# Layer-0 attention: PSUM banks shared two and two between scores and values, the turning of a group one slot later, the first half of the chain two slots later

## The chip, the cores and the metric

The kernel runs on one core of one Trainium2 chip. The metric is the device time of one launch in microseconds (us), the median over the runs shown. In the text PE is TensorE (matmuls), DVE is VectorE, ACT is ScalarE, POOL is GpSimd and SP is SyncE, which here only issues DMAs.

## The reference

A two-layer transformer over x of 4 batches by 512 tokens by 256 features, everything in float32. What bears on the change is layer 0:

```python
h = _layernorm(x, axis=-1) * (1 + ca) + sa
x = x + ga * _L0_attn_ref(h, Wq, Wkv, Wo)      # 16 heads of 16, one shared k and v, causal softmax
h = _layernorm(x, axis=-1) * (1 + cb) + sb
x = x + gb * _L0_ffn_ref(h, router_weight, router_bias, expert_bias)   # softmax over 64, top 8
```

Layer 1 follows (an attention with 16 heads of 128, and a gated feed-forward whose weights are gathered from a table of 16 values). The change does not touch it.

## The kernel before, in words

**Slots.** Layer 0's attention is one software pipeline, written out by hand. The work of a batch is cut into 44 units: four groups of four heads (`NG`, `HG`), and 11 units per group (`GU`), each a block of scores of up to 128x512 for one, two or four heads. All engines walk through the same loop `for s in range((NB - 1) * SLOTS0 + AFTER + CHAIN)`; each round is a slot, and `at(s, lag, length)` gives the unit that a step with this lag has in slot `s`. Each engine runs its own instructions strictly in this order and waits on semaphores.

For unit `i`, in the slots after its own: slot 0, PE computes scores into one of `S_BANKS` (lines 1257 and 1259) and DVE takes the row maxima (964). After a group's 11 units DVE turns the maxima (973 to 977), and SP's DMAs put them beside q, so that they take part in the next product. Slot 16 (`TURN`): PE computes the same scores turned (1239 and 1240) into bank 2 or 3, and ACT takes exp (727). Slot 18 (`VALUE`): behind the last unit of a key block, PE multiplies with the values (1270) into bank 5; four such steps fill the bank for a group. Slot 19: ACT copies the full bank to `oRaw` (735). Slot 20: PE turns `oRaw` back into bank 5 (1279), DVE divides by the row sums and writes `oTok` (983 and 987), and counts the semaphore `oev0`. The next group's first value product waits for `oev0`, since it writes bank 5.

**The chain.** When a batch's units are done, its rest runs in the slots of the next batch: `after0(n, b)`, n = 0 to 48, with n = 0 in slot `AFTER` = 63 of the batch. I call these chain slots. Chain slot 44 of one batch is chain slot 0 of the next, so chain slots 44 to 48 share slots with 0 to 4. The steps of before are: PE turns `oTok` (2, line 1185), ACT and DVE split it into a high and a low part (3 and 4, lines 668 and 887), PE multiplies with Wo (6 and 7), DVE applies the gate and adds to x (8 and 9, lines 892 and 894), the layer norm's statistics follow (10 to 13, lines 298 to 315), ACT normalises (14, line 326), PE turns (16, line 335), ACT scales and rounds (17 and 18), DVE makes the low part (19), PE computes the router (22 and 23), DVE adds the bias (24), ACT takes exp (25), DVE finds the top 8 (27 to 29, up to line 923), PE turns the weights (32, line 1211) and multiplies with the experts' biases (35, line 1219), DVE adds to x (36 and 37), and layer 1's norm follows: DVE 38 to 41, ACT 42, PE 44, ACT 45 and 46, DVE 47, and in 48 ACT issues two DMAs that store the result (705 and 706). The next batch's norm and q, k, v (`pre0`) run in other slots of the same loop.

**The banks.** Eight PSUM banks: scores 0, 1 and 4; turned scores 2 and 3; values 5; projections and the chain 6 and 7. A score matmul waits until the bank's last reader is done:

```python
S_BANKS = (0, 1, 4)
pe.wait_ge(max0, max(b * SLOTS0 + i - 2, 0))      # maxima of the unit three before
if k == 0:
    pe.wait_ge(oev0, b * NG + g)                  # the group before is in oTok
```

## Time and profile before

| what | value |
| --- | --- |
| median of 3 runs | 1391.39 us (1390.34 to 1394.19) |
| the profiled execution | 1389.02 us |
| its span, first to last instruction | 1387.2 us |
| PE busy | 1233.8 us, 89% |
| DVE busy | 961.9 us, 69% |
| ACT busy | 706.6 us, 51% |
| mean granted clock of PE | 0.937 |

The profile is of one execution of its own. Its time differs from the span by 1.82 us, which lies before the first and after the last instruction. Layer 0's attention with its chain takes the time from about 38 us to 395 us; layer 1 takes the rest.

### The profile page before, as it was taken

How to read it: one execution, taken by the hardware profiler on the slowest of the kernel's cores; microseconds unless marked ns; L12 is line 12 of the kernel's file. 1: busy time of each engine (PE TensorE's matmuls, PEld its weight loads, DVE VectorE, ACT ScalarE, POOL GpSimd, SP SyncE). 2: the span in 40 equal slices, each digit the busy share in tenths (PEclk: the TensorE clock that was granted, in tenths of full speed). 3: DMA queues.
4: the chain of work that ended last, by engine and by line, in shares of the span. 5: the costliest groups of instructions: out<-in, count | busy, mean ns of one | idle time of the engine just before them, and what ended most of it. 6: DMA issues, size and time to landing. Idle time of an engine off the chain costs nothing.

```text
span 1387.2 us, 24480 instructions
## 1 busy us (share of the span) xinstructions
PE 1233.8 (89%) x7708; PEld 949.9 (68%) x7708; DVE 961.9 (69%) x2821; ACT 706.6 (51%) x1639; POOL 551.8 (40%) x509
## 2 busy tenths in 40 slices
PE   6889888886479999999999999999998999996998
PEld 5535454443357787786777877878877788775887
DVE  5766777774576867878768778677668676674553
ACT  3354654555346546456455465465564564562442
POOL 0200000000048988898889888887603100000000
PEclk9799898888579999999999999999999999998999
DMA  6411011002010011101102101002002000000000
GB/s 216 122 36 46 25 35 55 24 32 92 30 66 12 31 39 72 40 1 41 41 10 94 36 8 39 31 15 96 15 19 79 16 30 30 0 0 1 16 16 31
DMA packets 31887, 56.76 MB, mean 41 GB/s; under 512 B 7096, under 2 KB 23328, under 8 KB 31312
## 3 DMA queue, kind: packets, MB, share of 16 engines
q1 hardware_dynamic: 27696, 42.93, 9.3%
q0 software_dynamic: 2976, 8.90, 2.2%
q10 hardware_dynamic: 1152, 4.19, 0.8%
q8 instruction: 26, 0.43, 0.1%
q14 instruction: 37, 0.30, 0.1%
HBM read 44.23 MB, written 11.66 MB: 40 GB/s over the span
## 4 chain that ended last, share of the span: by engine, by line
PE 56%; DVE 27%; issue 9%; ACT 5%; DMA 1%; SPq 1%; DVEq 0%; ACTq 0%
PE bank L1357 10%; PE bank L1335 8%; PE bank L278 7%; PE bank L280 6%; PE bank L279 6%; DVE qkst L1018 5%; PE bank L1346 4%; DVE qk L1037 4%; PE bank L1325 3%; PE bank L1270 2%; DVE negmax L964 2%; PE bank L1239 2%; ACT hN L326 2%; DVE negmax L1050 1%; PE bank L335 1%
## 5 line engine op out<-in xcount | busy, mean ns | idle before, releaser
L574 POOL TENSOR_SCALAR gtmp<-gidx,lut 128x344 f32<-128x344 int32 (+2 forms) x210 | 302.3, 1440 | 21.3
L577 POOL TENSOR_TENSOR gacc<-gacc,gtmp 128x344 f32<-128x344 f32 (+2 forms) x210 | 182.8, 870 | 17.5
L1335 PE MATMUL bank<-kT,qT 128*128 128x128 f32 (+3 forms) x512 | 179.5, 441 | 9.2 <-ACT probs L778 9.2
L1357 PE MATMUL bank<-pT,v 128*128 128x128 f32 x1280 | 155.4, 277 | 12.2 <-ACT pT L771 12.2
L778 ACT ACTIVATE probs<-bank,negmax 128x128 f32<-128x128 f32 (+3 forms) x256 | 135.7, 530 | 50.1 <-DVE negmax L1050 47.4
L1050 DVE TENSOR_REDUCE negmax<-bank 128x1 f32<-128x128 f32 (+3 forms) x256 | 123.4, 484 | 52.0 <-PE bank L1336 50.6
L1357 PEld LDWEIGHTS bank<-pT,v 128*128 128x128 f32 x1280 | 148.0, 192 | 15.9 <-DVE oL L1060 15.9
L964 DVE TENSOR_REDUCE negmax<-bank 128x1 f32<-128x512 f32 (+3 forms) x176 | 108.8, 635 | 68.2 <-PE bank L1259 67.3
L1018 DVE BATCH_NORM_STATS2 qkst<-qk 128x6 f32<-128x128 f32 x512 | 110.2, 281 | 64.0 <-issue 64.0
L278 PE MATMUL bank<-wgH,hL 128*128 128x512 f32 x384 | 152.9, 398 | 0.1
L280 PE MATMUL bank<-wgH,hH 128*128 128x512 f32 x384 | 152.9, 398 | 0.0
L279 PE MATMUL bank<-wgL,hH 128*128 128x512 f32 x384 | 152.4, 397 | 0.0
L771 ACT ACTIVATE pT<-bank 128x128 f32<-128x128 f32 (+3 forms) x256 | 111.1, 437 | 50.5 <-PE bank L1346 50.4
L567 POOL DMA_DIRECT2D gidx<-in_idx_gate x4 | 2.2, 540 | 335.1 <-DMA h_saved<-wft 335.1
L1045 DVE TENSOR_SCALAR probs<-probs,rsum 128x128 f32<-128x128 f32 (+3 forms) x256 | 124.1, 485 | 7.9
L757 ACT ACTIVATE qk<-bank 128x512 f32<-128x512 f32 x128 | 76.6, 599 | 98.9 <-PE bank L280 98.7
L1346 PE MATMUL bank<-identf,probs 128*128 128x128 f32 x640 | 112.7, 278 | 9.9 <-DVE probs L1045 6.7
L1346 PEld LDWEIGHTS bank<-identf,probs 128*128 128x128 f32 x640 | 69.9, 141 | 57.4 <-issue 28.0
L727 ACT ACTIVATE pT<-bank 128x384 f32<-128x384 f32 (+1 forms) x112 | 58.5, 535 | 84.1 <-PE bank L1240 78.9
L1037 DVE TENSOR_TENSOR qk<-qk,sm 128x512 f32<-128x512 f32 x128 | 98.2, 836 | 0.5
L1060 DVE TENSOR_TENSOR oL<-bank,oH 128x512 fp32r<-128x512 f32 x64 | 44.1, 689 | 74.5 <-ACT oH L785 74.3
L1335 PEld LDWEIGHTS bank<-kT,qT 128*128 128x128 f32 x512 | 77.3, 191 | 16.6 <-ACT probs L778 14.3
(215 smaller groups left out, 2713.6 us busy)
## 6 DMA issues: line engine op xcount, KB each, us to landing
hH<-h_saved SPq DMA_DIRECT2D x16, 512.0 KB, 3.9
hL<-h_saved SPq DMA_DIRECT2D x16, 512.0 KB, 4.6
qst<-q_parts SPq DMA_DIRECT2D x96, 64.0 KB, 2.3
wg<-in_wqkv SPq DMA_DIRECT2D x4, 1536.0 KB, 8.0
gate<-gates POOLq DMA_DIRECT2D x4, 512.0 KB, 7.4
wo<-in_wo SPq DMA_DIRECT2D x4, 512.0 KB, 8.9
out<-x SPq DMA_DIRECT2D x8, 256.0 KB, 2.1
wmod<-in_wmod SPq DMA_DIRECT2D x1, 1536.0 KB, 11.0
```

Of the source, the lines that this page charges most:

```text
L278: pe.matmul(o, wL, mH, start=start, stop=False)
L279: pe.matmul(o, wH, mL, start=False, stop=False)
L280: return pe.matmul(o, wH, mH, start=False, stop=stop)
L574: link(pool.tensor_scalar(tmp if j else acc, part, float(j), lut1[0:rows, j:j + 1], ALU.is_equal, ALU.mult))
L577: link(pool.tensor_tensor(acc, acc, tmp, ALU.add))
L964: dve.tensor_reduce(negmax[:, to:to + (heads - 1) * QT + 1:QT], bank[S_BANKS[(b * SLOTS0 + i) % 3]][:, 0:heads * w].rearrange("p (h k) -> ...
L1018: last = dve.bn_stats(qkst[:, u * HG + h, :], qk[:, u // 2, u % 2, h * HD1:(h + 1) * HD1])
L1037: dve.tensor_tensor(rows, rows, r.to_broadcast([P, HG, HD1]), ALU.mult).then_inc(qk_norm, 1)
L1050: dve.tensor_reduce(negmax[:, i:i + 1], bank[SCORE_BANKS[i % 3]][:, 0:n], AX.X, ALU.max, negate=True).then_inc(max1, 1)
L1335: pe.matmul(bank[SCORE_BANKS[i % 3]][:, 0:n], qT[:, h, t * P:n], kT[:, h, 0:n], start=True, stop=False)
L1346: last = pe.transpose(bank[5 + i % 2][:, k * P:(k + 1) * P], probs[:, i % 4, k * P:(k + 1) * P], identf[:, :])
L1357: last = pe.matmul(bank[7][:, t * P:(t + 1) * P], v1[:, k, h * HD1:(h + 1) * HD1], pT1[:, h % 2, at:at + P], start=(k == 0), stop=(k == t))
```

## The change

It does four things. (1) The third score bank, 4, becomes a second value bank: `S_BANKS = (0, 1)`, `V_BANKS = (5, 4)`, and groups alternate. A score matmul now waits for the maxima of the unit two before, and a group's first value product for the `oTok` of the group two before. (2) PE turns a group one slot later (`TAKEN` = 21, it was 20) and DVE writes `oTok` in slot 22; ACT's copy stays in slot 19. (3) The chain's first half comes two slots later, up to the router; the exp and norm of ACT are shifted by two or three, the top 8 by one. From chain slot 32 on nothing moves. (4) The wait for `cols_ready`, which guards bank 4's first use, goes from the third score to the second group's first value product.

```diff
-S_BANKS = (0, 1, 4)
+S_BANKS = (0, 1)
+V_BANKS = (5, 4)
 VALUE = TURN + 2
+TAKEN = VALUE + 3
...
-                if n == 3:
+                if n == 5:
                     act.wait_ge(y0_pe, b * 2)
...
-                        act.activation(oRaw[:, :], bank[5][:, :], ACT.Copy).then_inc(o_copied, 1)
+                        act.activation(oRaw[:, :], bank[V_BANKS[g % 2]][:, :], ACT.Copy).then_inc(o_copied, 1)
...
-                for i, b in at(s, VALUE + 2, SLOTS0):
+                for i, b in at(s, TAKEN + 1, SLOTS0):
                     if i % GU == GU - 1:
                         g = i // GU
                         dve.wait_ge(o_turned, b * NG + g + 1)
-                        pv = bank[5][:, :].rearrange("p (t h d) -> p t h d", t=QT, d=VW)
+                        pv = bank[V_BANKS[g % 2]][:, :].rearrange("p (t h d) -> p t h d", t=QT, d=VW)
...
-                    if b == 0 and i == 2:
-                        pe.wait_ge(cols_ready, 4)
-
-                    pe.wait_ge(max0, max(b * SLOTS0 + i - 2, 0))
-                    to = bank[S_BANKS[(b * SLOTS0 + i) % 3]][:, 0:heads * w].rearrange("p (h k) -> p h k", h=heads)
+                    pe.wait_ge(max0, max(b * SLOTS0 + i - 1, 0))
+                    to = bank[S_BANKS[(b * SLOTS0 + i) % 2]][:, 0:heads * w].rearrange("p (h k) -> p h k", h=heads)
...
                         g, k = i // GU, ENDS[i % GU]
+                        to = bank[V_BANKS[g % 2]]
                         if k == 0:
-                            pe.wait_ge(oev0, b * NG + g)
+                            pe.wait_ge(oev0, max(b * NG + g - 1, 0))
+                        if b == 0 and g == 1 and k == 0:
+                            pe.wait_ge(cols_ready, 4)
...
-                for i, b in at(s, VALUE + 2, SLOTS0):
+                for i, b in at(s, TAKEN, SLOTS0):
                     if i % GU == GU - 1:
...
-                            last = pe.transpose(bank[5][:, t * P:(t + 1) * P], oRaw[:, t * P:(t + 1) * P], identf[:, :])
+                            last = pe.transpose(bank[V_BANKS[i // GU % 2]][:, t * P:(t + 1) * P], oRaw[:, t * P:(t + 1) * P], identf[:, :])
```

The chain slots of `after0` move as the second hunk's does; in full:

| engine | step | before | change |
| --- | --- | --- | --- |
| PE | turn `oTok` | 2 | 4 |
| ACT, DVE | split it | 3, 4 | 5, 6 |
| PE, DVE | Wo; gate and add | 6, 7; 8, 9 | 8, 9; 10, 11 |
| DVE | norm | 10 to 13 | 12 to 15 |
| ACT | normalise | 14 | 17 |
| PE, ACT, DVE | turn; scale, round; low part | 16; 17, 18; 19 | 18; 19, 20; 21 |
| DVE | gate on `hN` | 20, 21 | 22, 23 |
| PE, DVE, ACT | router; bias; exp | 22, 23; 24; 25 | 24, 25; 26; 27 |
| DVE | top 8 | 27, 28, 29 | 28, 29, 30 |

No instruction is added or removed on any engine; only their order and the banks differ.

**PE, chain slot 44 of the first batch's chain.** L1279 (L1281 in the change) turns a batch's last group, L335 (L337) turns the rows of layer 1's norm, L1239 to L1259 (L1241 to L1258) are a slot's turned scores and scores. Before:

```order
L1257 MATMUL bank4<-kst,qst 128x256 x2
L1259 MATMUL bank4<-maskb,identb 128x2x128
L1279 MATMUL bank5<-identf,oRaw 128x128 x4
L335 MATMUL bank6<-identf,hN 128x128 x4
L335 MATMUL bank7<-identf,hN 128x128 x4
L1239 MATMUL bank2<-qst,kst 128x384
L1240 MATMUL bank2<-maskT,identb 128x128
```

In the change:

```order
L1256 MATMUL bank1<-kst,qst 128x256 x2
L1258 MATMUL bank1<-maskb,identb 128x2x128
L337 MATMUL bank6<-identf,hN 128x128 x4
L337 MATMUL bank7<-identf,hN 128x128 x4
L1241 MATMUL bank2<-qst,kst 128x384
L1242 MATMUL bank2<-maskT,identb 128x128
L1256 MATMUL bank0<-kst,qst 128x256 x2
L1258 MATMUL bank0<-maskb,identb 128x2x128
L1281 MATMUL bank4<-identf,oRaw 128x128 x4
```

The norm's eight matmuls now stand ahead of the group's turning, which comes a slot later and from another bank.

**ACT, at the second batch's chain.** L668 (L670) rounds the turned `oTok`, L705 and L706 (L707 and L708) issue the stores of the chain before, L727 (L729) is the exp of a slot. Before:

```order
L668 ACTIVATE oH0<-bank6 128x512
L668 ACTIVATE oH0<-bank7 128x512
L727 ACTIVATE pT0_1<-bank3 128x384
L705 DMA h1_saved<-hH 128x1024
L706 DMA h1_saved<-hL 128x1024
L727 ACTIVATE pT0_2<-bank2 128x512
```

In the change:

```order
L707 DMA h1_saved<-hH 128x1024
L708 DMA h1_saved<-hL 128x1024
L729 ACTIVATE pT0_2<-bank2 128x512
L670 ACTIVATE oH0<-bank6 128x512
L670 ACTIVATE oH0<-bank7 128x512
```

The two stores, with the wait for the low part ahead of them, now stand in front of the copies to `oH0`; before they stood behind.

**DVE, the first batch's layer norm.** L114 to L116 and L315 (L116 to L118 and L317) are the last steps of the norm, L973 to L977 (L975 to L979) the turning of a group's maxima, L964 (L966) the row maxima. Before, the end of the norm and what follows:

```order
L964 TENSOR_REDUCE negmax<-bank1 128x4
L114 TENSOR_TENSOR sm<-sm 128x4
L115 SCALAR_TENSOR_TENSOR sm<-sm 128x4
L116 SCALAR_TENSOR_TENSOR sm<-sm 128x4
L315 SCALAR_TENSOR_TENSOR sm<-mv,sm 128x4
L964 TENSOR_REDUCE negmax<-bank4 128x1
L973 CAST nmp<-negmax 128x16
L974 TENSOR_TENSOR nmp<-negmax,nmp 128x16
L977 STREAM_TRANSPOSE nmt<-nmp 128x32
```

In the change, a part in the middle of the norm:

```order
L966 TENSOR_REDUCE negmax<-bank1 128x1
L975 CAST nmp<-negmax 128x16
L976 TENSOR_TENSOR nmp<-negmax,nmp 128x16
L979 STREAM_TRANSPOSE nmt<-nmp 128x32
L116 TENSOR_TENSOR sm<-sm 128x4
L117 SCALAR_TENSOR_TENSOR sm<-sm 128x4
L118 SCALAR_TENSOR_TENSOR sm<-sm 128x4
L116 TENSOR_TENSOR sm<-sm 128x4
L117 SCALAR_TENSOR_TENSOR sm<-sm 128x4
L118 SCALAR_TENSOR_TENSOR sm<-sm 128x4
L966 TENSOR_REDUCE negmax<-bank0 128x1
```

The turning of the maxima was behind the norm's last instruction and now lies inside the norm.

## Rows read from the trace of the kernel before

**Rows 1.** Page of before: the span, TensorE's busy share, TensorE's granted clock in 40 slices.

```profile
span 1387.2 us, 24480 instructions
...
PE 1233.8 (89%) x7708; PEld 949.9 (68%) x7708; DVE 961.9 (69%) x2821; ACT 706.6 (51%) x1639; POOL 551.8 (40%) x509
...
PEclk9799898888579999999999999999999999998999
```

**Rows 2.** Busy time by stretch: us from:to, length, engines' busy us, PEclk, DMA share, GB/s.

```profile
80.00:117.50 37.50, 34.18 (x270) 19.06 (x268) 25.86 (x53) 22.72 (x43) 0.00 (x0) 1.00 0.13 36
...
199.50:271.30 71.80, 59.06 (x424) 32.30 (x424) 52.35 (x145) 36.66 (x77) 0.00 (x0) 0.86 0.12 38
...
215.60:228.10 12.50, 8.42 (x61) 4.01 (x57) 11.88 (x39) 5.77 (x12) 0.00 (x0) 0.81 0.05 15
```

**Rows 3.** Who waited for whom, 38 to 345 us: total us, times, longest us.

```profile
PE bank L1279 <- ACT oRaw L735: 14.8, 12, 6.0
...
PE bank L1270 <- DVE oTok L987: 6.9, 5, 1.9
...
PE bank L335 <- ACT hN L326: 5.3, 3, 1.8
...
PE bank L1257 <- DVE negmax L964: 4.1, 6, 1.5
```

**Rows 4.** TensorE in time order, 199 to 231 us: start, us, engine, line; idle before, releaser.

```profile
199.66 1.12 PE L1279 MATMUL bank<-identf,oRaw 128*128 128x128 f32 x4 [2.72 <-ACT oRaw L735]
...
210.78 0.39 PE L278 MATMUL bank<-w0H,oL 128*128 128x256 f32 x1 [1.06 <-DVE oL L887]
...
218.22 0.66 PE L1279 MATMUL bank<-identf,oRaw 128*128 128x128 f32 x4 [0.34 <-ACT oRaw L735]
...
222.14 1.06 PE L1270 MATMUL bank<-probs,vS 128*32 128x512 f32 x8 [1.91 <-DVE oTok L987]
...
228.10 1.97 PE L335 MATMUL bank<-identf,hN 128*128 128x128 f32 x8 [1.84 <-ACT hN L326]
```

**Rows 5.** TensorE in time order, 86 to 107 us, a turning.

```profile
91.80 0.66 PE L1279 MATMUL bank<-identf,oRaw 128*128 128x128 f32 x4 [0.34 <-ACT oRaw L735]
```

**Rows 6.** ScalarE in time order, 264 to 272 us: normalised rows, then the group's copy.

```profile
268.35 2.07 ACT L326 ACTIVATE hN<-x,sm 128x256 f32<-128x256 f32 x4 [3.44 <-DVE sm L315]
...
270.81 0.58 ACT L735 ACTIVATE oRaw<-bank 128x512 f32<-128x512 f32 x1
```

**Rows 7.** TensorE in time order, 210 to 218.5 us: first matmul of slots 8 and 10.

```profile
214.46 0.39 PE L1239 MATMUL bank<-qst,kst 98*128 98x512 bf16 x1
...
216.59 0.39 PE L1239 MATMUL bank<-qst,kst 98*128 98x512 bf16 x1
```

**Rows 8.** ScalarE in time order, 205 to 229 us: issues of the two stores.

```profile
208.96 0.39 ACTq L705 DMA_DIRECT2D h_saved<-hH  x1
209.38 0.49 ACTq L706 DMA_DIRECT2D h_saved<-hL  x1
```

**Rows 9.** VectorE in time order, 215 to 227 us: start and end of its long run.

```profile
215.64 0.68 DVE L892 TENSOR_TENSOR ytmp<-bank,gate 128x512 f32<-128x512 f32 x1
...
220.79 0.67 DVE L964 TENSOR_REDUCE negmax<-bank 128x2 f32<-128x512 f32 x1
...
225.72 0.16 DVE L315 SCALAR_TENSOR_TENSOR sm<-mv,sm 128x4 f32<-128x4 f32 x1
...
226.40 0.16 DVE L973 CAST nmp<-negmax 128x16 bf16<-128x16 f32 x1
...
226.81 0.21 DVE L977 STREAM_TRANSPOSE nmt<-nmp 128x32 bf16<-128x32 bf16 x1
```

**Rows 10.** TensorE in time order, 218 to 224 us: a score matmul with its mask.

```profile
219.62 0.40 PE L1257 MATMUL bank<-kst,qst 96*128 96x128 bf16 x4
```

**Rows 11.** VectorE in time order, 240 to 259 us: end of the top-8 work.

```profile
249.46 0.43 DVE L923 TENSOR_TENSOR ex<-ex,rsm 128x260 f32<-128x260 f32 x1
```

**Rows 12.** TensorE in time order, 240 to 275 us: turning of the routing weights.

```profile
251.14 0.60 PE L1211 MATMUL bank<-identf,ex 128*65 128x128 f32 x4
```

More of the change, by code:

```diff
@@ L676, in after0 @@
                     norm_f0.act_mod(act, b)
-                elif n == 18:
+                elif n == 20:
                     act.wait_ge(h1_stored, b * 32)
                     norm_f0.act_high(act, b, hH)
-                elif n == 19 and last:
+                elif n == 21 and last:
                     split_w1(0, 0, 3 * KT)
-                elif n == 25:
+                elif n == 27:
                     act.wait_ge(r_nmax, b + 1)
@@ L883, in after0 @@
                 last = b == NB - 1
-                if n == 4:
+                if n == 6:
                     for k in range(KT):
@@ L894, in after0 @@
                     ch.step(dve.tensor_tensor(xb(b, 2 * t2, 2), xb(b, 2 * t2, 2), ytmp[:, :, :], ALU.add))
-                elif n in (10, 11, 12, 13):
-                    for part in (2 * (n - 10), 2 * (n - 10) + 1):
+                elif n in (12, 13, 14, 15):
+                    for part in (2 * (n - 12), 2 * (n - 12) + 1):
                         norm_f0.dve_part(part, dve, ch, b)
-                elif n == 19:
+                elif n == 21:
                     norm_f0.dve_low(dve, b, hH, hL)
-                elif n in (20, 21):
-                    rows = hN[:, 2 * (n - 20):2 * (n - 20) + 2, :]
+                elif n in (22, 23):
+                    rows = hN[:, 2 * (n - 22):2 * (n - 22) + 2, :]
                     ch.mark(dve.tensor_tensor(rows, rows, gate(gate0, 1, b).to_broadcast([P, 2, D]), ALU.mult))
-                elif n == 24:
+                elif n == 26:
                     dve.wait_ge(r_pe, b + 1)
@@ L924, in after0 @@
                                       ALU.mult).then_inc(r_w, 1)
-                elif n == 30 and last:
+                elif n == 31 and last:
                     split_w1(0, slice(0, 3 * KT))
@@ L1269, in _ @@
                         for h in range(HG):
-                            last = pe.matmul(bank[5][h * VW:(h + 1) * VW, k * P:], vS[:, b * QT + k, :], pT0[k][:, h, :],
+                            last = pe.matmul(to[h * VW:(h + 1) * VW, k * P:], vS[:, b * QT + k, :], pT0[k][:, h, :],
                                              start=(k == 0), stop=(k == QT - 1))
                         last.then_inc(pv0, 1)
-                for i, b in at(s, VALUE + 2, SLOTS0):
+                for i, b in at(s, TAKEN, SLOTS0):
                     if i % GU == GU - 1:
```

30 lines of the change are left out of this document (15 added, 15 removed).

## The prediction

> **What bounds the kernel now.** The page comes first [rows 1]. PE is busy for 89% of 1387.2 us, but its granted clock reads 9 in nearly all slices from the thirteenth on and 5 to 8 in eight of the first twelve. The change lies wholly in the first 395 us, so I read that part by stretches [rows 2]. From 80 to 117.5 us, where no chain runs yet, PE is busy for 34.18 of 37.50 us at clock 1.00: there PE bounds. From 199.5 to 271.3 us, one batch of slots with a chain beside it, PE is busy for 59.06 of 71.80 us at clock 0.86, DVE for 52.35, ACT for 36.66. No engine is full. Something in turn bounds, so the waits are next.
>
> The list of waits [rows 3] shows what the change aims at: PE waited 14.8 us for ACT's copy `oRaw` ahead of the turning, 6.9 us for `oTok` ahead of a value product, and 5.3 us for normalised rows. For the third score bank's reader, `negmax`, it waited only 4.1 us. Of the 14.8 us one wait is 6.0 long and lies in the tail, where the last batch has nothing to run beside it.
>
> Where each wait sits decides what it is worth. In time order [rows 4] I see three sorts. (a) A turning waits 0.34 us because the copy was issued only one slot before. (b) At 199.66 us the turning waits 2.72 us: it is chain slot 44, ACT was held by the norm and the copy stands behind it. (c) At 222.14 a value product waits 1.91 us for `oTok`, and at 228.10 PE waits 1.84 us for normalised rows. Sort (c) lies in a stretch in which DVE is busy for 11.88 of 12.50 us [rows 2]: from the gate at 215.64 to the end of the norm at 225.88 (225.72 + 0.16) DVE runs without a gap [rows 9], and PE is busy for 8.42 us only. There DVE bounds, and a shorter wait at one place comes back at the next.
>
> **The change part by part.**
>
> (1) *Turning one slot later, early groups.* Two groups are turned between 80 and 117.5 us, with 0.34 us of wait each, of which one is shown [rows 5]. PE bounds there, so 2 x 0.34 = 0.7 us go. Of the other seven short waits three lie in DVE's long run and are worth nothing; the rest are inside the balance of the chain below.
>
> (2) *Chain slot 44.* The norm's turning now precedes the group's. ACT ends the normalising at 270.42 (268.35 + 2.07) and the copy at 271.39 (270.81 + 0.58) [rows 6]. PE may go on 1.0 us sooner; what is left of the wait is for the normalised rows. This place occurs twice (199.7 and 271.4 us) outside the tail. In the tail the same 1.0 us is gained before `oH0`, but there the stores now precede `oH0` on ACT (below, 0.9 us), so I count the tail at zero.
>
> (3) *The first half of the chain, two slots later.* For one period I add up how much later the first Wo product and the gate behind it come. Two more slots precede them: from the start of chain slot 8 to that of 10 PE took 216.59 - 214.46 = +2.1 us [rows 7]. The wait for `oL0`, -1.06 [rows 4], goes, since DVE's low part of the other chain no longer stands right ahead of it. On ACT the two stores, 0.39 + 0.49 = +0.9 [rows 8], now stand ahead of the copies to `oH0`, and the slot's exp behind these. That makes 2.1 - 1.06 + 0.9 = +1.9. What queues behind the stores is one exp and the copies; PE's turned scores wait for that exp.
>
> (4) *The turning of the maxima inside the norm.* It took DVE from 226.40 to 227.02 (226.81 + 0.21), 0.6 us [rows 9], behind the norm; now it lies inside, so the norm ends +0.6 later. SP's DMAs of the maxima are no later by slots.
>
> (5) *What is given back.* From slot 32 on nothing moved, so two slots less lie between the norm's turning and the weights' turning (L1211). If only PE counted, -2.1 would come back, and with them a part of ACT's wait on its exps. A limit is the router's chain. The top 8 ended at 249.89 (249.46 + 0.43) [rows 11], L1211 began at 251.14 [rows 12]: slack 1.25 us. The bounds are thus -1.25 (slack alone) and -3.0 (both slots, the 0.34 at the turning and some 0.5 of better packing on ACT). I take -2.6, nearer the full return, because the router's scores leave the slots in which DVE also had the second group's `oTok`.
>
> (6) *Two score banks.* Unit s now waits for the maxima of s - 2. In DVE's long run this binds: the score matmul at 219.62 [rows 10] was issued while the maxima two units before ended at 221.46 (220.79 + 0.67) [rows 9], so it will start 1.8 us later. But PE then waited until 222.14 for `oTok`, a wait that is gone. The one takes the place of the other, value 0. Outside DVE's run I allow +0.2 per period; bounds 0 and the 1.84 us of this one instance. `cols_ready` costs nothing, since the columns are copied long before the second group's values. The first twelve units, which start behind DVE's opening work, are bound by DVE at either depth: 0, at most +0.4.
>
> *The sum.* Full period: -1.0 + 1.9 + 0.6 - 2.6 + 0.2 = -0.9, twice: -1.8. The first period (117.5 to 199.5 us) has neither the wait at 44 nor the stores nor the wait for `oL0`: +2.1 + 0.6 - 2.6 + 0.2 = +0.3. With (1): -1.8 + 0.3 - 0.7 = **-2.2 us**. The profiled execution took 1389.02 us, so it would be 1386.8; the median of the runs shown is 2.37 higher, so for the median 1391.39 - 2.2 = **1389.2 us**. A measurement of this kernel tells about 0.3%, 4.2 us, from no change. So I forecast no difference that can be told.
>
> *A rule against the trace.* The trace says that most of the wait for `oTok` sits where DVE bounds [rows 2, 4] and is worth nothing. The Trainium skill (Perfetto Trace Analysis, Matmuls) says that independent matmul groups should rotate through different PSUM banks, so that the reading of one overlaps the next group. By that rule the values gain a rotation and the scores keep a shorter one. By the trace the sum has 0 for this, by that rule -6.9. The trace agrees that the values stood still behind one bank; it cannot show the scores with two.
>
> **The rivals.**
>
> *PE was the bound after all, faster.* If the waits that bank 5 causes are worth their face, this happens: 6.9 us for `oTok`, the waits before the turnings outside the tail, 14.8 - 6.0 = 8.8, together 15.7 us [rows 3]; PE would further hold its full clock longer. Half of it, as DVE covers half, gives 1391.4 - 7.9 = 1383.5 us. For it: PE is the busiest engine in the period (59.06 against 52.35) and at the lower of its two levels (1.2 GHz) for part of the time, which a steadier feed would change; 0.81 in the long run is where it waits. Against it: DVE's run without a gap, which the change lengthens. The rule named above would bring the time out this way. Chance 0.30.
>
> *The two slots aren't given back, slower.* The mechanism: the chain to the top 8 is a serial one, router, bias, exp, top 8. If it takes all the slots that it has, PE stands before L1211 for what the first half lost. The price per period: (3) + (4) = +2.5, less the slack of 1.25, = +1.3, plus the score banks' full +1.84, less 1.0 at slot 44 in two of three: 3 x 3.1 - 2.0 - 0.7 = +6.7, 1398.1 us. It decides when less than about 2 us return, and more so if score waits leave DVE without work after its run. For it: fourteen slots now lie between the norm's turning and L1211 where sixteen were, and each holds maxima of 0.6 us beside the chain's DVE work. Against it: DVE was busy only 52.35 of 71.80. Chance 0.22.
>
> **How the numbers follow.** The forecast, no difference that can be told, has 0.48 around 1389.2, its own range 1386 to 1394. The rival on the fast side has 0.30, the one on the slow side 0.22. Each spreads a little over the bound at 1387.2 or 1395.6: faster by over 0.3% 0.33, within 0.3% 0.45, slower 0.22. The range for 8 in 10 reaches from 1382.5 (the fast rival and 1 us) to 1397.5 (nearly the slow one).
>
> **What would show it.** In the changed profile the turnings' waits for `oRaw` should be near nothing outside the tail, and those for `oTok` gone. In their place PE's waits for `negmax` grow from 4.1 to some 10 us, most of them in DVE's long run, which stays about 11 us long with the turning of the maxima inside. At chain slot 44 PE waits for normalised rows 1.0 us less than it did for the copy. The wait of PE before L1211 (none now) becomes 0 to 1.5 us. The period from one chain slot 44 to the next stays within 1 us of 71.8. I would be wrong if DVE's run shows gaps, if the wait before L1211 is over 2 us, or if the clock of the period leaves 0.84 to 0.88.

## Result and the profile after

| what | before | change |
| --- | --- | --- |
| median | 1391.09 us (6 runs, 1390.25 to 1394.19) | 1398.87 us (6 runs, 1397.28 to 1399.76) |
| ratio, 95% interval | | 1.0051 [1.0038, 1.0063] |
| the profiled execution, its span | 1389.02, 1387.2 us | 1397.76, 1396.0 us |
| layer 0's last store issued, from the span's start | 393.7 us | 398.9 us |

The change makes the kernel slower, by 7.8 us or 0.51%. That is more than the 4.2 us that can be told from nothing, and it lies outside the range of the prediction (1382.5 to 1397.5).

The page of the change, against [rows 1] (TensorE's clock in the last row):

```profile
span 1396.0 us, 24479 instructions
...
PE 1230.8 (88%) x7708; PEld 941.1 (67%) x7708; DVE 965.9 (69%) x2821; ACT 705.7 (51%) x1639; POOL 552.3 (40%) x509
...
PEclk8799988998579999999999999999999999998999
```

The span is 8.8 us longer, PE is busy for 3.0 us less and DVE for 4.0 more. Neither engine's work has grown by what the span has, so most of the loss is waiting. The stretches that answer to [rows 2] (length, then PE, PEld, DVE, ACT and POOL busy, then PEclk, DMA share and GB/s):

```profile
80.00:117.50 37.50, 35.17 (x286) 18.47 (x278) 26.78 (x55) 24.67 (x48) 0.00 (x0) 1.00 0.13 35
204.50:276.30 71.80, 59.25 (x431) 31.43 (x428) 53.17 (x145) 36.37 (x75) 0.00 (x0) 0.90 0.11 37
```

From 80 to 117.5 us, where no chain runs, PE is busy for 35.17 us where it was for 34.18, with 286 matmul records for 270: it gets through more work in the same time. In a period (204.5 us is 5 us behind 199.5, as the change is at that place) PE is busy for 59.25 us as before (59.06), but at clock 0.90, where it was 0.86. The list of waits from 38 to 345 us, against [rows 3]:

```profile
PE bank L1256 <- DVE negmax L966: 28.1, 32, 1.9
...
PE bank L1241 <- DMA qst<-nmt: 7.3, 6, 1.7
...
PE bank L337 <- ACT hN L328: 7.0, 3, 5.5
...
PE bank L337 <- DVE rsm L910: 1.8, 1, 1.8
```

The 14.8 us for `oRaw` and the 6.9 for `oTok` are gone from the list, as intended. The waits for `negmax` rose from 4.1 to 28.1, far more than the 10 forecast. The 7.3 us for the DMA of the maxima (`nmt`) are no larger than before, where that row, which did not stand among those shown, reads 7.5. The sum alone doesn't tell where these waits lie, and one has moved to a costly place. The list therefore doesn't explain the loss. What does is to follow the ends of the same steps through both traces. Read from TensorE's rows, in us, as the end of the step's last matmul, the change less before (before's own time in the second column):

| end of the step | before | change | late chain, old banks | Wo in slot 7 | hFA later | both repairs | norm turned first |
| --- | --- | --- | --- | --- | --- | --- | --- |
| chain 1: Wo | 136.2 | +3.5 | +4.3 | +0.6 | +3.6 | +0.8 | +0.6 |
| chain 1: router | 162.7 | +4.3 | +5.7 | +3.5 | +4.4 | +3.0 | -1.1 |
| chain 1: weights turned | 173.6 | +6.3 | +8.8 | +6.9 | +1.8 | +0.5 | -1.0 |
| chain 1: norm turned (slot 44) | 202.5 | +5.0 | +8.8 | +6.3 | +0.5 | -2.5 | -3.6 |
| chain 2: Wo | 214.6 | +10.2 | +13.3 | +7.5 | +6.5 | -1.1 | -0.3 |
| chain 2: router | 241.2 | +11.0 | +14.1 | +10.4 | +6.2 | +1.8 | -3.1 |
| chain 2: weights turned | 251.7 | +8.6 | +11.8 | +8.9 | +3.8 | -0.6 | -3.1 |
| chain 2: norm turned (slot 44) | 274.3 | +5.8 | +11.6 | +6.9 | +1.9 | -3.4 | -4.9 |
| chain 3: Wo | 286.4 | +9.0 | +16.4 | +7.9 | +7.2 | -3.2 | -4.1 |
| chain 3: router | 313.0 | +8.7 | +16.8 | +10.4 | +7.7 | -1.0 | -4.6 |
| chain 3: weights turned | 322.0 | +5.9 | +14.0 | +7.9 | +5.3 | -3.8 | -4.6 |
| layer 0: last norm turned | 390.7 | +5.2 | +14.9 | +7.2 | +3.7 | -4.5 | -6.6 |

(The last five columns are the experiments `c_late_chain`, `h_wo7`, `j_pre3`, `k_pre3_wo7` and `m_turn_after`, below. Each column is one execution, and executions of one kernel differ: those of the controls q_before_wo7 and r_before_pre3, whose medians can't be told from before's, end layer 0 4.0 and 4.3 us ahead of before's. So a sum down a column says little to within some 4 us; a step that recurs in many executions says more.)

Two places stand out. **Up to Wo** the change loses 5.2 us in chain 2 (from +5.0 to +10.2) and 3.2 in chain 3; some 2.1 of that are the two slots that now precede Wo, and are due back later. **From the router to the turning of the weights** it gives back 2.4 and 2.7 us in chains 2 and 3, as forecast, but loses 2.0 in chain 1.

A second table leaves the moved steps out. The mask's matmul of a slot's turned scores (L1240, L1242 in the change) is in the same slot in every version. How much longer than in before it took from one such matmul to another, in us, in one execution of each:

| chain, slots | change | a | c | f | h | j | k | m | q | r |
| --- | --- | --- | --- | --- | --- | --- | --- | --- | --- | --- |
| chain 2, 5 to 11 | +2.5 | 0.0 | +2.5 | +2.5 | 0.0 | +2.5 | +0.1 | +1.6 | -0.2 | 0.0 |
| chain 3, 5 to 11 | +1.0 | +1.5 | +2.5 | +2.5 | +0.1 | +1.0 | +0.1 | 0.0 | -0.3 | 0.0 |
| chain 1, 11 to 25 | -0.6 | -1.6 | -0.1 | +3.8 | -0.7 | -0.6 | -1.4 | -1.6 | -1.1 | -1.1 |
| chain 2, 11 to 25 | -0.7 | -2.8 | -0.7 | +3.4 | -0.7 | -1.7 | -0.7 | -2.8 | +0.2 | -2.3 |
| chain 1, 25 to 35 | +5.6 | +1.2 | +6.7 | +1.0 | +8.5 | +1.9 | +1.9 | 0.0 | 0.0 | +1.1 |

(The letters are the experiments below.) The first row of the change, from before's slots 5 and 11, then its own: 10.28 us became 12.77.

```profile
207.04 0.27 PE L1240 MATMUL bank<-maskT,identb 128*128 128x256 bf16 x1
...
217.32 0.22 PE L1240 MATMUL bank<-maskT,identb 128*128 128x128 bf16 x1
```

```profile
212.60 0.27 PE L1242 MATMUL bank<-maskT,identb 128*128 128x256 bf16 x1
...
225.37 0.22 PE L1242 MATMUL bank<-maskT,identb 128*128 128x128 bf16 x1
```

*The first place.* TensorE of the change in time order, around chain slot 8 of the second chain (start, us; in brackets the idle time before and its releaser):

```profile
206.40 1.06 PE L337 MATMUL bank<-identf,hN 128*128 128x128 f32 x8 [0.41 <-ACT hN L328]
...
216.04 0.22 PE L1258 MATMUL bank<-maskb,identb 128*128 128x128 bf16 x1
217.92 0.39 PE L1241 MATMUL bank<-qst,kst 98*128 98x512 bf16 x1 [1.66 <-DMA qst<-nmt]
...
219.51 0.58 PE L280 MATMUL bank<-w0H,oL 128*128 128x256 f32 x1
...
222.03 0.28 PE L282 MATMUL bank<-w0H,oH 128*128 128x256 f32 x1
222.15 0.39 PE L1241 MATMUL bank<-qst,kst 98*128 98x512 bf16 x1
```

PE has finished the slot's last score matmul at 216.26 us and waits until 217.92, because the turned scores of chain slot 8 are the first of a group (unit 11 plus the turn's 16 slots) and need the maxima that SP's DMAs bring. Behind them stands Wo. In before, Wo stood ahead of this wait, in slots 6 and 7. VectorE's turning of the maxima, of before and of the change:

```profile
207.54 0.21 DVE L977 STREAM_TRANSPOSE nmt<-nmp 128x32 bf16<-128x32 bf16 x1
```

```profile
212.22 0.21 DVE L979 STREAM_TRANSPOSE nmt<-nmp 128x32 bf16<-128x32 bf16 x1
```

In the change they are turned at 212.43 (212.22 + 0.21) and usable at 217.92, 5.5 us later. In before they were turned at 207.75; 5.5 us on would be 213.2, when PE was at Wo (210.78 to 214.6), and the turned scores at 214.46 [rows 7] waited for nothing. Wo covered this wait, and the change has pulled the cover away. After the wait the clock is low as well. The granted clock is the third number from the end; first the change, then before at Wo:

```profile
216.20:219.50 3.30, 1.64 (x14) 0.45 (x12) 1.87 (x4) 1.60 (x4) 0.00 (x0) 0.86 0.65 211
219.50:222.10 2.60, 2.60 (x16) 2.59 (x12) 0.00 (x0) 0.00 (x0) 0.00 (x0) 0.52 0.07 24
222.20:224.60 2.40, 2.40 (x25) 1.86 (x24) 0.56 (x1) 0.60 (x1) 0.00 (x0) 1.00 0.00 0
```

```profile
210.80:214.40 3.60, 3.60 (x28) 3.25 (x28) 1.67 (x3) 0.86 (x2) 0.00 (x0) 1.00 0.52 203
```

PE was busy for 1.64 of 3.30 us, the clock was granted at 0.86, and then Wo's first half ran at 0.52, nearly all at the lower level of 1.2 GHz. Its twelve products took 2.64 us (219.51 to 222.15), where in before they took 1.53 (210.78 to 212.31) at 1.00: +1.1. The Trainium skill (TensorE: Matmul & The Clock Gate, A second HAM failure mode) reports such falls for a kernel that cycled through PSUM banks with small idles between groups; here the trace agrees that an idle stood ahead of the fall, but the idle is for a DMA and not for a bank.

The fall is not a fixed companion of the wait. In all profiles, chains 2 and 3, Wo's first half ran at a clock of 0.50 to 0.67 in eight of ten places where Wo stood in slots 8 and 9, at 0.51 to 0.68 in four of sixteen where it stood in 6 and 7, and at 1.00 in all ten where it stood in 7 alone. In chain 3 of the change it ran at 1.00, and there slots 5 to 11 cost 1.0 us in place of 2.5. So the lost cover costs 1.0 us by itself, and 1.5 more where the clock falls.

*The second place.* Chain 1 meets the q, k, v norm of batch 3 (its steps are `pre0`; `hA` and `hFA` are its tiles; L345 scales it, L687 is the router's exp). First ScalarE, then VectorE, then TensorE of the change:

```profile
170.78 0.60 ACT L729 ACTIVATE pT<-bank 128x512 f32<-128x512 f32 x1 [2.95 <-PE bank L1242]
171.27 1.44 ACT L345 ACTIVATE hFA<-bank,modc 128x512 f32<-128x512 f32 x2
172.60 0.35 ACT L687 ACTIVATE ex<-lg,rsm 128x64 f32<-128x64 f32 x1
```

```profile
168.67 0.42 DVE L910 TENSOR_REDUCE rsm<-lg 128x4 f32<-128x256 f32 x1
...
174.06 0.61 DVE L914 MAX8 top<-ex 128x8 f32<-128x64 f32 x4 [1.70 <-ACT ex L687]
```

```profile
169.35 1.07 PE L337 MATMUL bank<-identf,hA 128*128 128x128 f32 x8 [1.77 <-DVE rsm L910]
...
179.22 0.65 PE L1213 MATMUL bank<-identf,ex 128*65 128x128 f32 x4 [0.61 <-DVE ex L925]
```

In before, ScalarE at the same place:

```profile
165.13 0.34 ACT L685 ACTIVATE ex<-lg,rsm 128x64 f32<-128x64 f32 x1
...
167.31 1.44 ACT L343 ACTIVATE hFA<-bank,modc 128x512 f32<-128x512 f32 x2
```

In before the exp (165.13) stood ahead of `hFA` (167.31). In the change the router's maximum, DVE's L910, is two slots later. PE's turning of `hA`, which uses the chain's banks and so waits for it, loses 1.77 us; the units behind it come late; ACT scales `hFA` first and takes the exp at 172.60, 3.5 us after the maximum was there (168.67 + 0.42); and DVE waits 1.70 us for it. On unmoved work the change loses 5.6 us there, from slot 25 to 35, and 1.1 and 0.1 us in the same slots of chains 2 and 3. No other chain meets these steps: only chain 1, the first batch's, has a batch's `pre0` begin in its slots 26 to 29, and that is batch 3's.

### The profile page after: what moved, and what is told of

Same layout as the page of the kernel before. It is cut to its first block, busy times and chain, and to the rows that moved or that the text cites. A ratio compares the mean times of both kernels' runs of the same rounds, so it can differ in the third digit from the quotient of the medians.

```text
span 1396.0 us, 24479 instructions
## 1 busy us (share of the span) xinstructions
PE 1230.8 (88%) x7708; PEld 941.1 (67%) x7708; DVE 965.9 (69%) x2821; ACT 705.7 (51%) x1639; POOL 552.3 (40%) x509
## 4 chain that ended last, share of the span: by engine, by line
PE 53%; DVE 29%; issue 10%; ACT 5%; DMA 1%; SPq 1%; DVEq 0%; ACTq 0%
PE bank L1359 10%; PE bank L1337 7%; PE bank L280 7%; PE bank L281 6%; PE bank L282 6%; DVE qkst L1020 4%; DVE qk L1039 4%; PE bank L1348 4%; PE bank L1327 2%; DVE negmax L966 2%; PE bank L1272 2%; DVE negmax L1052 1%; PE bank L1256 1%; PE bank L1241 1%; PE bank L337 1%
## 5 line engine op out<-in xcount | busy, mean ns | idle before, releaser
L966 DVE TENSOR_REDUCE negmax<-bank 128x1 f32<-128x512 f32 (+3 forms) x176 | 109.7, 638 | 69.8 <-PE bank L1258 68.6
L729 ACT ACTIVATE pT<-bank 128x384 f32<-128x384 f32 (+1 forms) x112 | 59.2, 538 | 79.3 <-PE bank L1242 72.1
L1256 PE MATMUL bank<-kst,qst 96*128 96x512 bf16 (+3 forms) x256 | 69.1, 323 | 28.6 <-DVE negmax L966 28.1
```

The lines of the kernel that those rows point to most:

```text
L966: dve.tensor_reduce(negmax[:, to:to + (heads - 1) * QT + 1:QT], bank[S_BANKS[(b * SLOTS0 + i) % 2]][:, 0:heads * w].rearrange("p (h k) -> ...
```

## The experiments

All times are medians; the ratio is to runs of before that were measured beside it, with its 95% interval. In the expectations, LATE CHAIN holds the chain's slots to blame, TWO SCORE BANKS the waits for `negmax`, PHASE the clock; COVER is the first place above, ROUTER and COLLISION are theories of the second.

**a_old_chain.** The change's banks and later turning, the chain in its old slots. The diff, against the change, shows two of the steps; all go back.

```diff
-                if n == 5:
+                if n == 3:
...
-                elif n in (8, 9):
+                elif n in (6, 7):
```

> The change with its banks and its later turning, but the chain in the slots of before. Theory LATE CHAIN (the two slots and what they collide with cost the time): the cost is gone and the gain at chain slot 44 stays, 1386 to 1390 us, at or under before (1391.1). Theory TWO SCORE BANKS (the scores' shorter rotation costs it): 1396 to 1399 us, as the change. Theory PHASE (layer 1 took 3.6 us more in the profile, by when TensorE's clock fell): 3 us or more of any difference lies behind 400 us of the profile.

Measured: 1391.93 us (12 runs), 0.9994 [0.9981, 1.0008]. The loss is gone; the gain expected on top of that, 1386 to 1390, can't be seen in the time. Banks and turning alone do nothing that can be told, in spite of this row of its waits:

```profile
PE bank L1256 <- DVE negmax L966: 27.6, 34, 1.9
```

**b_two_score.** Only the third score bank taken away; of the diff the banks are shown, and the score's wait goes with them, from i - 2 to i - 1.

```diff
-S_BANKS = (0, 1, 4)
+S_BANKS = (0, 1)
```

> Before with two score banks and nothing else; bank 4 stands idle. TWO SCORE BANKS: slower by 4 to 7 us, 1395 to 1398. LATE CHAIN: within 1.5 us of before, with at most 2 us lost in the first 60 us of slots, where the profile of the change shows the scores waiting for maxima.

Measured: 1393.39 us (12 runs), 1.0011 [0.9995, 1.0027]. At most some 3.8 us, and the best value is 1.4.

```profile
PE bank L1257 <- DVE negmax L964: 24.0, 36, 1.9
```

PE waits 24.0 us for `negmax`, 20 more than before, and the time moves by 1.4: the waits stand where DVE or something behind it bounds anyway. TWO SCORE BANKS falls.

**c_late_chain.** Before with the change's chain slots, banks and turning as they were; of the diff against before one step is shown.

```diff
-                if n == 3:
+                if n == 5:
```

> Before with the chain's first half in the slots of the change, banks and turning as before. LATE CHAIN: slower by 4 to 7 us, 1395 to 1398, and in the profile the router's exp of the first chain stands 3 us behind the maxima it needs, since ACT has the next batch's scaling ahead of it. TWO SCORE BANKS: 1390 to 1392.

Measured: 1404.37 us (6 runs), 1.0083 [1.0065, 1.0101]. The later chain alone costs 12.3 us, more than the whole change and twice what was expected. With it, banks and turning give some 4.5 us (by the ratios) to 5.5 us (by the medians) back, which without it are worth nothing.

**d_ex26.** The change, with ACT's router exp one slot earlier (27 to 26), ahead of `hFA`.

```diff
-                elif n == 27:
+                elif n == 26:
                     act.wait_ge(r_nmax, b + 1)
```

> The change with ACT's router exp at chain slot 26, where it stands ahead of the scaling for batch 3. LATE CHAIN: 3 us less than the change, 1395.5 to 1396.5, all of it between 168 and 180 us of the profile. TWO SCORE BANKS: within 1 us of the change (1398.9).

Measured: 1400.35 us (6 runs), 1.0055 [1.0037, 1.0073]. A miss: no gain at all. The exp of chain 1 came 4 us sooner than in the change (168.54 for 172.60), but the top 8 began only 1.1 sooner and the weights were turned 0.4 sooner. I take it that this puts right only what follows PE's wait for the maximum, not that wait.

**e_wo_old** and **h_wo7.** The change with Wo ahead of the DMA's wait again: in e with all its steps from the turning of `oTok` to Wo in their old slots, in h with only the two halves of Wo in slot 7.

```diff
-                elif n in (8, 9):
+                elif n == 7:
                     pe.wait_ge(ot_lo, (b + 1) * KT)
-                    for t in (2 * (n - 8), 2 * (n - 8) + 1):
+                    for t in range(QT):
```

> The change with the turning and splitting of oTok and the Wo products back in chain slots 2, 3, 4, 6 and 7; gate, norm and router stay late. Theory COVER (Wo in slots 6 and 7 filled the wait for the DMAs of the maxima, which gate slot 8's turned scores; in 8 and 9 it stands behind that wait): most of the 7.8 us comes back, 1391 to 1394 us. Theory ROUTER (the loss is made where the late router meets the norm of batch 3 and the top 8): 1397 to 1399 us. Theory PLAIN (each of the two slots costs its own work before Wo, and only that): 1394 to 1396 us.

> The change with both halves of Wo in chain slot 7, ahead of the turned scores that wait for the DMAs; nothing else moves, oTok is still turned in slot 4. COVER: 4 us or more less than the change, at or under 1395 us, and the wait for the DMAs at slot 8 is gone from the second and third chain. PLAIN and ROUTER: within 1.5 us of the change, 1397.5 to 1400.

Measured: e 1396.59 us, 1.0038 [1.0022, 1.0053]; h 1396.77 us, 1.0038 [1.0022, 1.0054] (12 runs each). Both lie some 2 us under the change, which their intervals alone don't separate from it, and in no range that a theory had named: less than COVER's, more than the others'. The traces show the mechanism. TensorE of h, where Wo begins, and its waits for that DMA:

```profile
219.05 0.38 PE L280 MATMUL bank<-w0H,oL 128*128 128x256 f32 x1 [0.85 <-DVE oL L889]
```

```profile
PE bank L1242 <- DMA qst<-nmt: 3.1, 3, 1.1
```

The wait for the DMA (L1242 in h is the change's L1241) falls from 7.3 to 3.1 us, and from slot 44's norm to Wo the second chain loses 1.3 us instead of 5.2. On unmoved work slots 5 to 11 cost 0.0 and 0.1 us in chains 2 and 3, in place of 2.5 and 1.0. Most of it was lost again elsewhere: chain 1's slots 25 to 35 cost 8.5 us in h for 5.6 in the change, and the gate, which reads Wo's product, still had its slots behind 9. Why the collision was dearer here is open.

**f_router_old** and **i_wo7_router.** The change (f) and h (i) with router, bias, exp and top 8 in their old slots.

```diff
-                elif n in (24, 25):
+                elif n in (22, 23):
                     norm_f0.wait_ready(pe, b)
```

> The change with router, bias, exp and top 8 back in slots 22 to 29; everything up to the low part stays late. ROUTER: 1391 to 1395 us, and in the profile the first chain's exp no longer falls behind. COVER: at most 3 us less than the change, 1396 to 1399 us.

> Both: Wo in slot 7 and the router in its old slots, banks and later turning as in the change. If COVER and ROUTER both hold, they add up: 1388 to 1392 us, at or under before. If only one holds, as the better of the two runs alone.

Measured: f 1405.32 us, 1.0104 [1.0079, 1.013] (6 runs); i 1399.38 us, 1.0054 [1.0028, 1.008] (7 runs). ROUTER's price falls, and i's forecast with it: f is slower than the change. From Wo to the turning of the weights the change gives 1.6 us back in chain 2; f loses 1.7 there and i 4.1, and chain 1 is no better than in the change (+2.7 in f for +2.8). The second table shows why. The collision itself is gone in f: slots 25 to 35 of chain 1 cost 1.0 us where they cost 5.6. But from slot 11 to 25 f loses 3.4 to 3.8 us in each chain, where the change loses none: the router now stands right behind the low part that it reads, and PE waits for it, a wait that the change doesn't have:

```profile
PE bank L280 <- DVE hL L357: 3.2, 3, 1.1
```

That wait is 1.1 us a chain; where the rest of the 3.4 to 3.8 goes is not followed. An early router thus cures the second place at a higher price. The difference of f and i, 5.9 us, is a second measure of COVER, in medians.

**j_pre3** and **k_pre3_wo7.** The change with batch 3's steps on `hFA` two slots later; k has Wo in slot 7 besides.

```diff
-                if n == 2:
+                if n == (4 if b == NB - 1 else 2):
...
-                elif n == 3:
+                elif n == (5 if b == NB - 1 else 3):
...
-                if n == 4:
+                if n == (6 if b == NB - 1 else 4):
...
-                if n == 1:
+                if n == (3 if b == NB - 1 else 1):
```

> The changed kernel; only the last batch's q, k, v norm, which runs beside the first chain, has its steps on hFA moved two slots later (PE's turning of norm_a0 1 to 3, ACT's scaling and rounding 2, 3 to 4, 5, DVE's low part 4 to 6). COLLISION theory (in the change these steps meet the router's maximum and exp, which moved two slots, and cost the first chain its give-back of about 4.4 us): some 3 to 4.5 us less than the change, about 1394.5 to 1396, and the distance from the first chain's router to its turning of the weights falls from 2.0 us more than before to about 2 us less. If the give-back is missing for another reason (the slots there are not filled by TensorE): no change from 1398.9.

> The same as j_pre3, and both halves of the Wo product in chain slot 7 instead of 8 and 9. If COVER (Wo stands ahead of the wait for the DMA of the maxima, as before, worth about 2 us by the earlier run) and COLLISION are two separate costs, they add: 1392 to 1394. If they are the same time seen twice: about the better of the two alone, 1394.5 to 1396.5.

Measured: j 1393.01 us, 1.0008 [0.9993, 1.0022]; k 1389.01 us, 0.9990 [0.9977, 1.0004] (12 runs each). Against 1398.87 these are -5.9 and -9.9 us (by the ratios -6.0 and -8.5), more than expected of either, and j's and k's intervals lie wholly under the change's. From j to k, measured side by side, Wo's place is worth 4.0 us by the medians and 2.5 by the ratios. In j, ScalarE and TensorE at the second place:

```profile
169.15 0.35 ACT L687 ACTIVATE ex<-lg,rsm 128x64 f32<-128x64 f32 x1 [0.58 <-DVE rsm L910]
...
171.61 1.44 ACT L345 ACTIVATE hFA<-bank,modc 128x512 f32<-128x512 f32 x2
```

```profile
174.73 0.65 PE L1213 MATMUL bank<-identf,ex 128*65 128x128 f32 x4 [0.46 <-DVE ex L925]
```

The exp is back ahead of `hFA`; ScalarE waits 0.58 us for the maximum and starts as soon as it is there, and the weights are turned 4.5 us sooner than in the change (174.73 for 179.22). From router to weights chain 1 now gives 2.6 us back (+4.4 to +1.8 in the table), as the others did in the change. COLLISION holds. In k chain 2's Wo stands at -1.1 where it stood at +10.2.

**m_turn_after** and **n_last_late.** Two ways to have the norm turned ahead of the last group at chain slot 44 in the kernel before. In m PE does a slot's chain step before its group turning; in n only the last group is turned, and written to `oTok`, a slot later. The expectation of m says that it differs only at chain slot 44. That is not so: a group is turned in chain slot 22 as well, and there m puts the first half of the router ahead of it.

```diff
+                for n, b in at(s, AFTER, CHAIN):
+                    after0(n, b)
                 for i, b in at(s, VALUE + 2, SLOTS0):
...
-                for n, b in at(s, AFTER, CHAIN):
-                    after0(n, b)
```

> The kernel before; on TensorE the turning of a group stands behind the chain's step of the same slot instead of ahead of it. This differs only at chain slot 44, where layer 1's norm is then turned ahead of the batch's last group. It takes this one part out of the change. By the prediction's step (2): 1.0 us less at each of two places, and the same once in the tail, so 1388.5 to 1390.5 against 1392. By the change's profile, in which this segment came out 2.6 us shorter: up to 5 us less, 1387. If the gain at slot 44 needs the later slot as well: no difference.

> The kernel before; only a batch's last group is turned, and written to oTok, one slot later (three banks for scores, one for values, chain in its old slots). The 2.7 us wait for the copy at chain slot 44 goes, and what is left is the wait for the normalised rows. By what the change gained at this place (2.6 us, twice outside the tail): 1387 to 1389 against 1392. By step (2) of the prediction (1.0 us, twice): about 1390. If the next group's first value product, which then waits for oTok one slot longer, takes the gain back: 1391 to 1393.

Measured: m 1386.89 us, 0.9964 [0.9951, 0.9978] (13 runs); n 1390.64 us, 0.9993 [0.9979, 1.0008] (12 runs). m is faster than both kernels, by 4.9 us than before. TensorE at chain slot 44, of m, then of before; and the stretches' granted clock, of m (the last at its second chain's Wo), then of before, then of the change:

```profile
197.76 1.06 PE L335 MATMUL bank<-identf,hN 128*128 128x128 f32 x8 [1.85 <-ACT hN L326]
198.66 1.06 PE L1284 MATMUL bank<-identf,oRaw 128*128 128x128 f32 x4
```

```profile
200.57 1.91 PE L335 MATMUL bank<-identf,hN 128*128 128x128 f32 x8
```

```profile
197.70:199.30 1.60, 1.54 (x11) 1.51 (x12) 1.53 (x3) 1.37 (x3) 0.00 (x0) 0.82 0.04 10
199.30:202.00 2.70, 2.70 (x15) 1.59 (x14) 2.19 (x5) 1.81 (x4) 0.00 (x0) 0.50 0.00 0
...
208.90:211.60 2.70, 2.69 (x12) 2.62 (x12) 1.16 (x2) 0.30 (x1) 0.00 (x0) 0.51 0.63 250
```

```profile
199.60:202.30 2.70, 2.64 (x13) 2.58 (x14) 2.24 (x5) 0.49 (x2) 0.00 (x0) 0.50 0.02 6
```

```profile
206.40:208.30 1.90, 1.90 (x18) 1.78 (x19) 1.83 (x4) 1.87 (x5) 0.00 (x0) 1.00 0.04 9
```

The wait is 0.87 us shorter (1.85 for 2.72 [rows 4]), near the 1.0 forecast. The clock adds nothing here. In before the eight matmuls of the norm took 1.91 us, at 0.50, in m 1.06, at 0.82; but in m the full fall to 0.50 comes right behind them, on the work that before did at 0.90. On unmoved work, from chain slot 39 to slot 5 of the next chain, m gains 0.8 us and n, whose wait is the same 1.85, 0.9: the wait and no more. By slot 11 both have lost 1.6 us again, because the clock is low at Wo's first half too (0.51 in m), behind the same wait of 1.06 us for `oL0` after which before's stood at 1.00.

What m has and n has not is the turning in slot 22. From slot 21 to 23 m gains 0.52 us in each of the three chains, 1.6 in all, and so does s, which has the same edit; n gains nothing there. By these parts, two places of 0.85 us and three of 0.52, m's edit is worth some 3.3 us and what the tail adds, and n's 1.7; at the second slot 44, though, the traces with this order spread from -2.7 to +0.4 us with the clock. m's profile is of its fastest run, 1378.43 us, 8.5 under its median, so its column overstates.

**o_late_fixed, q_before_wo7, r_before_pre3, s_best.** Do the two repairs undo what the later chain did, or help any kernel? o has both on c_late_chain, q and r one each on before. s is m with r's edit.

> The kernel before (three banks for scores, one for values, turning in its old slot) with the change's chain slots, and both repairs: Wo's two halves in chain slot 7, the last batch's steps on hFA two slots later. Without repairs this kernel took 1404.4. If COVER and COLLISION are what a later chain costs with any banks: it loses about what the change lost by the two repairs, 9.9, so 1394 to 1396, with the rest above before from the copy at chain slot 44 that is still waited for. If the repairs need the second value bank or the later turning: 1398 or more.

> A control: the kernel before with both halves of Wo in chain slot 7 (they stood in 6 and 7, both ahead of the wait for the maxima's DMA already). If the gain of this repair in the change comes from the order against that wait: no gain here, 1391 to 1394. If two halves in one slot are better by themselves: 1388 to 1390.

> A control: the kernel before with only the last batch's steps on hFA two slots later. In before, the router's maximum and exp stand ahead of these steps, so there is nothing to repair. If the 5.9 us that the same edit gave the change are a COLLISION made by moving the router: no gain here, 1391 to 1393.5. If these steps are better two slots later in any case: 1386 to 1389.

> The kernel before with the norm turned ahead of the last group in chain slot 44 (it took 1386.9) and the last batch's steps on hFA two slots later. If the control r_before_pre3 shows no gain, this shows none over 1386.9 either, and it is a second measurement of the version that beats both kernels: 1385.5 to 1388.5. If the steps on hFA are worth something in before: 1382 to 1385.

Measured (12 runs each, before 1393.41): o 1394.71 us, 1.0019 [1.0004, 1.0034]; q 1390.83, 0.9991 [0.9974, 1.0009]; r 1391.57, 0.9993 [0.9974, 1.0011]; s 1389.47, 0.9985 [0.9967, 1.0003]. On the late chain with old banks the repairs take the ratio from 1.0083 to 1.0019, 0.64% or 8.9 us. On before neither does anything that can be told. They repair a damage that only the later chain does. s was meant to confirm m too, and stands above its expected range: it gives 0.15% where m gave 0.36%, and its interval just reaches no gain. The best values for m's edit are thus 2 and 5 us, and one of two measurements tells it from nothing.

## Why the prediction was wrong

The sum was -2.2 us; the change is +7.8. By steps:

*(1) Early turnings, -0.7.* Right, and a little small: both waits are gone, and on unmoved work each of the two turnings gives 0.53 us, -1.1 in all, in the change as in a. The wait of 0.34 us was not the whole price of a turning that stands too early.

*(2) Chain slot 44, -1.0 twice.* Right for the wait, too small for the change. The change's segment is 2.6 and 2.7 us shorter (+7.6 at the end of the norm's arithmetic to +5.0 when it is turned; and +8.5 to +5.8); on unmoved work, slot 39 to slot 5 of the next chain, it gains 2.0 and 2.6. m and n, and also d, h, j, k and s, which have the same order, gain 0.8 to 0.9 at the first of these places, and in all seven the clock was low behind it. In the change it stayed at 1.00, where before's was 0.50. The sum had nothing for that, and it can't be counted on.

*(3) The first half of the chain, +1.9.* **This is the first step that failed.** It came to +5.2 in chain 2 and +3.2 in chain 3. Without the two slots' own 2.1 the forecast was -0.2; on unmoved work slots 5 to 11 measured +2.5 and +1.0, and 0.0 and 0.1 with Wo back in slot 7. I read the two slots' +2.1 off TensorE's rows, where slots 8 and 9 follow each other without a wait, and did not ask why slot 8 had none. The parts of chain 2: two slots +2.1, wait for `oL0` -1.06 (right, it is gone), the DMA +1.66, Wo at the lower clock +1.1, two waits for `negmax` +1.05 (0.27 and 0.78), the last group's turning, now behind the norm's, +0.43, a wait of 0.56 for `pT` gone; together +4.7 of 5.2. The stores' +0.9 on ACT did not show. The prediction says under (4) that "SP's DMAs of the maxima are no later by slots". That was true, and beside the point: the consumer had not moved either, but the work that hid the wait had.

*(4) The maxima's turning inside the norm, +0.6.* Right. VectorE's run in the change, its end:

```profile
236.69 0.16 DVE L317 SCALAR_TENSOR_TENSOR sm<-mv,sm 128x4 f32<-128x4 f32 x1
```

From 225.83 to 236.85 it takes 11.0 us without a gap, against 10.2 before [rows 9], as forecast. From Wo's end to the norm's end each chain takes 0.8 us more (12.05 for 11.26 us).

*(5) Given back, -2.6.* Right for chains 2 and 3 (-2.4 and -2.7). **Wrong for chain 1, the second step that failed:** +2.0 there, 4.6 us off. The sum took the first period to differ from the others only by what its start lacks. It looked at what the moved steps meet in `after0` and never at batch 3's `pre0`, whose first steps share slots 26 to 29 with chain 1 alone.

*(6) Two score banks, +0.2 per period, at most +0.4 in the opening.* The periods were right, the opening was not. At the eleventh unit's turned scores (70.78 us in before) all ten executions with two score banks stand 5.4 to 7.2 us behind before's, the seven others with three -0.3 to +2.3. At the seventeenth it is 1.5 to 3.2 against -2.6 to +1.9: most is made up, but on average some 3 us remain, of which the early turnings later return 1.1. The loss in the time is less: b measures 1.4 us in all, at most 3.8. The waits for `negmax` exceed my 10 us by 18, and cost little.

*The Trainium skill's rule.* The Trainium skill (Perfetto Trace Analysis, Matmuls) says that independent matmul groups should rotate through different PSUM banks. Going by it, the sum would have had -6.9 us. With the chain in its old slots the second value bank and the later turning give 0.9994 [0.9981, 1.0008]. The trace was the better guide: the waits for bank 5 were not worth their face. Only with the later chain is there a gain, from c to the change.

*The rivals.* "PE was the bound" gave 1383.5 and is out. "The two slots aren't given back" gave 1398.1, and 1398.9 was measured, but the time is right by luck, for other reasons. Its serial chain before L1211 did not bind: the waits there (L1213) are 0.6 us in chains 1 and 2 and 0.3 in chain 3, inside my 0 to 1.5. Two of three chains gave back in full. Its full 1.84 us per period for the score banks was not there. "The clock tips" did not come as an average (the period's clock rose to 0.90, outside the 0.84 to 0.88 I named) but at single places: +1.5 around Wo in chain 2, and over 1 us to the good at each slot 44.

*What isn't settled.* In the table the change loses 5.2 us in layer 0; its profiled span is 8.8 longer. The other 3.6 lie in layer 1, which the change doesn't touch: 3.0 of them in one of its rounds, at some 1065 to 1128 us. The profiles of a, b, d and e show some 3 there too, that of c none, so it goes with neither the chain nor the loss. Nor does it go with the kernel: r_before_pre3's profile ends layer 0 4.3 us before before's and its span is 0.2 us shorter, so 4.1 more lie in layer 1. In before PE's low-clock stretch of the round named ends at 1070 us, in the change it lies from 1072 to 1079. I take it that the clock's ups and downs fall on other work when all in front of them shifts, but no run tests this. How much of the 7.8 us is lost in which layer is therefore not shown; that the two places cost it is, by the medians of a, j, k and of f and i. Of the 9.9 us that both repairs remove, the single executions show 9.7 in layer 0, but k's profile is of its fastest run, 3.8 us under its median.

With both repairs the change takes 0.9990 [0.9977, 1.0004] of before's time, and the sum was -2.2 us, 0.9984. The sum fits a kernel in which Wo still covers the DMA and no norm stands in the way, but in part by luck: it also lacks what slot 44 gave beyond its 1.0 and what the opening cost, and these have opposite signs.

## What to carry to other kernels

When steps are moved in a hand-ordered pipeline, look at the waits that are zero before: ask of each wait that the moved work passes (a DMA's above all) whether that work was what hid it. Then lay the new slots of every moved step beside all other work of those slots, for each period by itself, the first and the last too, since one collision in one period can cost what all the others save. When one step is swapped with another, compare on work that neither touches: a step that merely comes first looks like a gain. A list of waits by their sums says little: here 24 us more for the score banks cost almost nothing, and 7.3 instead of 7.5 for a DMA hid most of one loss, because one wait had moved to where nothing ran beside it.

## What was not expected of the hardware

A wait can cost twice, but need not. After 2.7 us of idle TensorE before did 2.7 us of matmuls at 0.50, and the norm's turning took 1.91 us where it took 1.06 in the change at 1.00; after 1.66 us of waiting for a DMA twelve products took 2.64 for 1.53 us. But ahead of the second chain's Wo before and m_turn_after both waited 1.06 us, and the products behind ran at 1.00 in one and at 0.51 in the other. A gain of clock at one place can also be paid back at the next, as in m. And executions of one kernel differ by more than such gains: 35 runs of before measured together spread from 1384.5 to 1395.1 us, another 35 from 1386.8 to 1394.4, so that 2 us are told only by many runs or by stretches that recur in many traces.
